# Six banks and spare products for the last pass of layer 3, run alone at the end of a four-layer kernel

## The chip, the cores and the metric

The kernel runs on one core of a Trainium2 chip. The core has five engines with a queue each: TensorE (PE; its weight loads are listed as PEld), VectorE (DVE), ScalarE (ACT), GpSimd (POOL) and SyncE (SP, here a queue of DMAs). Each queue is worked off strictly in the order in which the program was written; engines wait for one another by semaphores. The metric is the time of one execution in microseconds (us) on the device. TensorE's clock has two levels, 1.2 and 2.4 GHz; the profile shows the granted level as "PEclk", where 1.00 is 2.4 GHz and 0.50 is 1.2 GHz.

## The reference, cut to what matters

Four layers run one after the other on 64 sequences of 64 positions and 256 features. Layers 0 to 2 are attention layers (the last with a feed-forward part); layer 3 is a recurrent one:

```
xa  = ln(x); sx = shift(xa) - xa
xxx = tanh((xa + sx*maa_x) @ maa_w1)             # "maa"
xm_j = xa + sx*(maa_j + xxx_j @ maa_w2[j])       # "mix 0" to "mix 4": decay w, k, v, r, g
w   = exp(-exp(decay + tanh(xw@td_w1)@td_w2))    # "td", "decay"
k, v, r = xk@Wk.T, xv@Wv.T, xr@Wr.T;  g = silu(xg@Wg.T)
s_t = k_t v_t + w_t s_(t-1);  out_t = r_t (u k_t v_t + s_(t-1))   # "bonus", "scan"
x1  = x + groupnorm(out) * g @ Wo.T              # "center", "variance", "gate", "project"
xc  = ln(x1); xk2, xr2 = xc + sx2*ffn_k, xc + sx2*ffn_r
return x1 + sigmoid(xr2@Wfr.T) * (relu(xk2@Wfk.T)**2 @ Wfv.T)     # "ffn r", "ffn k", "ffn v"
```

All of it is in 32-bit floats.

## The kernel before, in words

The 64 sequences are worked in eight groups of eight (512 positions). Group g's layers 0 to 2 run in a block together with layer 3 of group g-1. The program of each engine is a list of steps of layers 0 to 2, and between them it calls `step()`, which emits the stages of layer 3 that are due there. Which stage is due at which step of which engine is a table written out by hand (`STAGES`, `PLACES`, `SCAN_PLACES`). The ninth block, number 8, has no group for layers 0 to 2 (`now` is None): each engine calls `rest()`, and layer 3 of the last group runs alone, stage after stage.

On TensorE the stages of layer 3 are, in order: turn, maa, mix 0, mix 1, td, k, mix 2, decay, v, mix 3, mix 4, r, g, bonus, 19 scan steps, center, variance, project, turn 2, ffn k, ffn r, ffn v. "maa" has four products of 128x512 (two of them in the first accumulation), a mix two products with a 32-row operand, td two, decay two with a 64-row operand, and k, v, r, g and ffn k four each. Project, ffn r and ffn v have eight products with 256 columns each. "turn" and "turn 2" are eight transposes of 128 columns. Every product in 32-bit floats is two MATMUL instructions in the profile (so four products are "x8"); a transpose is one.

TensorE's results go to eight PSUM banks, and the banks to rings (`RINGS`, line 71): "score" has banks 0 and 1, "turn" 2 to 5, "late" 6 and 7. `fill` takes the next bank of a ring for a tile, and waits until the tile that was there before has been read (`bank{b}_free`); the reader, ACT or DVE, waits for `bank{b}_full` in `take`. All of layer 3 goes through the ring "late", so a stage's third product waits until the first has been read. `product` (one or two accumulated products into one bank), `flip` (transposes) and `natural` (products with 256 columns, four to a bank) write a bank each.

Readers: ACT reads turn, maa, td, k, decay, v, r, g, center, variance, turn 2, ffn k and ffn r (mostly line 1047; L1090 for g, L1097 for center). DVE reads the mixes (L1307, then L1309 makes the mixed input xm), bonus, the scan's sums (L1334), project (L1387) and ffn v (L1408). The mixed inputs have two buffers. The stage g releases the DMAs of v (L666) that the scan needs; the scan itself is a chain between POOL (L1580), DVE (L1316, L1328) and a small product (L759).

Of the kernel before, what the change touches and what calls it, by code (L numbers as in the profile page):

```python
# [54 lines left out]
def build(nc, a, out):  # L55

    with ExitStack() as ctx:
# [5 lines left out]
        def sig(name):  # L63

            if name not in sems:
                sems[name] = ctx.enter_context(nc.semaphore(name))
            return sems[name]


        banks = [ctx.enter_context(nc.psum_tensor(f"bank{i}", [128, 512], F32)) for i in range(8)]  # L70
        RINGS = {"score": [0, 1], "turn": [2, 3, 4, 5], "late": [6, 7]}
        turns, fills, place, linked = {}, {}, {}, {}

        era = [None]
# [8 lines left out]
        def spot(tile):  # L83

            return place[era[0], tile]

        def fill(pe, ring, tile):

            b = RINGS[ring][turns.get(ring, 0) % len(RINGS[ring])]
            turns[ring] = turns.get(ring, 0) + 1  # L90
            n = fills.get(b, 0)
            if n:
                pe.wait_ge(sig(f"bank{b}_free"), n)
            fills[b] = n + 1
            place[era[0], tile] = (b, n + 1)
            return banks[b], sig(f"bank{b}_full")
# [430 lines left out]
        def clear_all():  # L527
# [60 lines left out]
        )  # L588
        due = {}
        for stage in STAGES:  # L590
            spots = SCAN_PLACES[stage[1]] if stage[0] == "scan" else PLACES[stage]
# [34 lines left out]
        def group_block(now, before, after):  # L626
# [45 lines left out]
            def tensor_program(pe):  # L672
# [3 lines left out]
                def product(tile, cols, terms, ring="turn"):  # L676

                    t, full = fill(pe, ring, tile)
                    for n, (lhsT, rhs) in enumerate(terms):
                        ins = mm(t[0:lhsT_cols(lhsT), 0:cols], lhsT, rhs, start=n == 0, stop=n == len(terms) - 1)  # L680
                    ins.then_inc(full, 1)

                def flip(tile, src, ring="turn"):

                    for k in range(KT):
                        t, full = fill(pe, ring, (tile, k))
                        for p in range(NP):
                            ins = tr(t[:, 128 * p:128 * p + 128], src[:, p, 128 * k:128 * k + 128], ident[:, :])
                        ins.then_inc(full, 1)

                def natural(tile, q, lhsT, rhs, ring="turn"):

                    t, full = fill(pe, ring, (tile, q))
                    for p in range(2):
                        for k, r in enumerate(rhs):
                            ins = mm(t[:, E * p:E * p + E], lhsT(2 * q + p, k), r, start=k == 0, stop=k == len(rhs) - 1)  # L696
                    ins.then_inc(full, 1)

                def layer3(stage):
                    def mix(f):  # L700
                        rows = slice(32 * (f % 4), 32 * (f % 4) + 32)
                        for m in range(KT):
                            product((stage, m), 512, [(maa2[rows, f // 4, 128 * m:128 * m + 128], xf[rows, f // 4, :])], "late")

                    def square(w, moving):
                        for m in range(KT):
                            product((stage, m), 512, [(wt[w][:, k, 128 * m:128 * m + 128], moving(k)) for k in range(KT)], "late")

                    def mixed(n, w):
                        pe.wait_ge(sig("xm_ready"), past("xm_ready") + KT * (n + 1))  # L710
                        square(w, lambda k: xm[:, (n + 1) % 2, k, :])

                    def project(w, moving):
                        for q in range(2):
                            natural(stage, q, lambda p, k: moving[:, k, 128 * p:128 * p + 128], [wt[w][:, k, :] for k in range(KT)], "late")

                    if stage == "turn":
                        pe.wait_ge(sig("xh3_ready"), past("xh3_ready") + NP)
                        flip(stage, xh3, "late")
                    elif stage == "maa":  # L720
                        pe.wait_ge(sig("x1m_ready"), past("x1m_ready") + KT)
                        product("maaA", 512, [(maa1[:, k, 0:128], xm[:, 0, k, :]) for k in range(KT)], "late")
                        product("maaB", 512, [(maa1[:, k, 128:160], xm[:, 0, k, :]) for k in range(KT)], "late")
                    elif stage[0:3] == "mix":
                        pe.wait_ge(sig("xf_ready"), past("xf_ready") + 2)
                        mix(MIXES[int(stage[4])])
                    elif stage == "td":
                        pe.wait_ge(sig("xm_ready"), past("xm_ready") + KT)
                        product("td", 512, [(td1[:, k, :], xm[:, 1, k, :]) for k in range(KT)], "late")
                    elif stage == "decay":  # L730
                        pe.wait_ge(sig("td_ready"), past("td_ready") + 1)
                        for m in range(KT):
                            product((stage, m), 512, [(td2[64:64 + DD, 128 * m:128 * m + 128], xf[64:64 + DD, 1, :])], "late")
                    elif stage == "k":
                        mixed(1, "Wk")
                    elif stage == "v":
                        mixed(2, "Wv")
                    elif stage == "r":
                        mixed(3, "Wr")
                    elif stage == "g":  # L740
                        mixed(4, "Wg")
                    elif stage == "bonus":
                        for k in range(KT):
                            pe.wait_ge(sig("ruk_ready"), past("ruk_ready") + k + 1)
                            product((stage, k), 512, [(heads8[:, :, :], ruk[:, k, :])], "late")
                    elif stage[0] == "scan":

                        n = stage[1] - 3
                        if 0 <= n < KT * HS and n % 2 == 1:
                            k, j = n // HS, n % HS  # L750
                            if j == 1:
                                t, full = fill(pe, "late", ("o3", k))
                            else:
                                b, c = spot(("o3", k))
                                t, full = banks[b], sig(f"bank{b}_full")
                            pe.wait_ge(sig("rs_ready"), past("rs_ready") + n + 1)
                            for i in (j - 1, j):
                                c, e = i % 4, i // 4
                                ins = mm(t[32 * c:32 * c + 32, :], pick[:, e, :, :], rs[:, i % RS, :], start=e == 0, stop=e == 1)  # L759
                            ins.then_inc(full if j == HS - 1 else sig("rs_used"), 1)  # L760
                    elif stage == "center":
                        for k in range(KT):
                            pe.wait_ge(sig("o3_ready"), past("o3_ready") + k + 1)
                            product((stage, k), 512, [(center8[:, :], ruk[:, k, :])], "late")
                    elif stage == "variance":
                        for k in range(KT):
                            pe.wait_ge(sig("sq_ready"), past("sq_ready") + k + 1)
                            product((stage, k), 512, [(same8[:, :, :], sq[:, k, :])], "late")
                    elif stage == "project":
                        pe.wait_ge(sig("ogT_ready"), past("ogT_ready") + KT)  # L770
                        project("Wo", ogT)
                    elif stage == "turn 2":
                        pe.wait_ge(sig("xh4_ready"), past("xh4_ready") + NP)
                        flip(stage, xh4, "late")
                    elif stage == "ffn k":
                        pe.wait_ge(sig("xk2_ready"), past("xk2_ready") + KT)
                        square("Wfk", lambda k: xk2[:, k, :])
                    elif stage == "ffn r":
                        pe.wait_ge(sig("xr2_ready"), past("xr2_ready") + KT)
                        project("Wfr", xr2)  # L780
                    elif stage == "ffn v":
                        pe.wait_ge(sig("kk_ready"), past("kk_ready") + KT)
                        project("Wfv", kkT)
# [928 lines left out]
```

## Time and profile before

| | us |
|---|---|
| median of 3 runs (lowest to highest) | 2005.09 (2001.06 to 2007.68) |
| the profiled execution | 2005.4 |
| its span | 2003.3 |
| PE busy (share of the span) | 1673.5 (84%) |
| DVE busy | 1275.2 (64%) |
| ACT busy | 931.7 (47%) |
| POOL busy | 801.7 (40%) |

The span is what the engines' records cover; 2.1 us lie around it. Times in the rows below are counted from the start of the span. An engine's busy share is a mean over parts of the program with different limits; the last 156 us, from 1847 on, are the block in which layer 3 runs alone.

### The profile page before, as it was taken

The page shows a single profiled execution, that of the slowest core. Times are in us where ns is not written, and L with a number is a line of the kernel's source. Part 1 is how long each engine was busy: PE and PEld are TensorE (multiplying, and loading weights), DVE is VectorE, ACT ScalarE, POOL GpSimd, SP SyncE. Part 2 cuts the span into 40 slices and gives each one's busy share as a digit, 9 for nine tenths or more (in the row PEclk, how much of TensorE's full clock was granted, in tenths as well). Part 3 has the DMA queues.
Part 4 walks back from the last instruction along what each step waited for, and adds up shares of the span by engine and source line. Part 5 has one row for each costly group of instructions (what it writes and reads, how often), then busy time and mean ns, then how long its engine had stood idle before and what let it go on. Part 6 is the DMA issues. An engine that isn't in the chain of part 4 may idle for free.

```text
span 2003.3 us, 36727 instructions
## 1 busy us (share of the span) xinstructions
PE 1673.5 (84%) x13614; PEld 1033.5 (52%) x13614; DVE 1275.2 (64%) x2181; ACT 931.7 (47%) x1831; POOL 801.7 (40%) x894
## 2 busy tenths in 40 slices
PE   3788898898988899798988989888987989888825
PEld 2465555564564645555555655546455555556203
DVE  3453468844796557854688457965589546883383
ACT  1555544545545444546445455454545454453202
POOL 3542137603474036611376024840367114760070
PEclk9899899999999999999989989999999999899757
DMA  6001005110241004210041102420042101410070
GB/s 175 1 2 35 1 7 59 24 41 4 29 49 38 18 1 54 34 27 18 10 56 23 38 7 25 52 39 18 1 55 34 27 18 14 52 24 12 0 85 11
DMA packets 73584, 60.92 MB, mean 30 GB/s; under 512 B 38961, under 2 KB 56513, under 8 KB 73409
## 3 DMA queue, kind: packets, MB, share of 16 engines
q1 hardware_dynamic: 49600, 41.70, 16.6%
q10 hardware_dynamic: 23264, 16.85, 3.0%
q8 instruction: 111, 1.82, 0.4%
q14 instruction: 65, 0.52, 0.1%
q0 software_dynamic: 544, 0.03, 0.0%
HBM read 20.28 MB, written 4.19 MB: 12 GB/s over the span
## 4 chain that ended last, share of the span: by engine, by line
PE 56%; ACT 15%; DVE 11%; issue 7%; POOL 6%; DMA 2%; ACTq 0%; DVEq 0%; POOLq 0%; SPq 0%
PE bank L680 24%; PE bank L819 6%; PE bank L1017 6%; PE bank L696 3%; PE bank L914 3%; PE bank L960 3%; ACT soft_ring L1156 3%; POOL soft_ring L1618 3%; DMA late<-late 2%; DVE late L1316 2%; PE bank L985 2%; PE bank L759 2%; ACT soft_ring L1175 2%; DVE soft_ring L1463 2%; ACT late L1047 2%
## 5 line engine op out<-in xcount | busy, mean ns | idle before, releaser
L1618 POOL TENSOR_TENSOR soft_ring<-soft_ring,seg_max 128x512 f32<-128x512 f32 x256 | 276.7, 1096 | 273.2 <-DVE seg_max L1469 272.5
L1175 ACT ACTIVATE soft_ring<-soft_ring 128x512 f32<-128x512 f32 x256 | 160.6, 627 | 228.5 <-POOL soft_ring L1618 216.0
L1580 POOL TENSOR_TENSOR late<-late 128x520 f32<-128x520 f32 x128 | 189.0, 1477 | 156.4 <-DMA late<-late 118.9
L1316 DVE TENSOR_TENSOR_SCAN late<-late 128x520 f32<-128x520 f32 x128 | 218.5, 1707 | 22.0 <-DVE xr L1494 6.7
L960 PE MATMUL bank<-ident,soft_ring 128*128 128x128 f32 x1024 | 170.0, 295 | 51.1 <-ACT soft_ring L1175 46.3
L1463 DVE SCALAR_TENSOR_TENSOR soft_ring<-bank,mask 128x512 f32<-128x512 f32 x256 | 164.2, 682 | 34.8 <-PE bank L819 25.7
L960 PEld LDWEIGHTS bank<-ident,soft_ring 128*128 128x128 f32 x1024 | 116.4, 147 | 135.0 <-ACT soft_ring L1175 83.7
L1469 DVE TENSOR_REDUCE seg_max<-soft_ring 128x8 f32<-128x512 f32 (+1 forms) x256 | 166.2, 675 | 6.2 <-DVE early L1527 2.0
L1626 POOL TENSOR_SCALAR soft_ring<-soft_ring,rden 128x256 f32<-128x256 f32 x64 | 61.6, 962 | 265.4 <-DVE rden L1436 265.4
L819 PE MATMUL bank<-early 64*128 64x512 f32 (+1 forms) x512 | 120.3, 556 | 56.4 <-ACTq L1159 53.6
L1047 ACT ACTIVATE late<-bank 128x512 f32<-128x512 f32 (+2 forms) x104 | 62.0, 596 | 204.4 <-PE bank L680 200.3
L680 PE MATMUL bank<-early,w 128*128 128x512 f32 x256 | 117.7, 610 | 17.9 <-ACT early L1234 17.9
L1589 POOL COPY late<-edge 128x8 f32<-128x8 f32 x16 | 3.2, 199 | 322.5 <-DVE late L1410 322.4
L680 PE MATMUL bank<-late,maa 32*128 32x512 f32 (+2 forms) x224 | 113.7, 631 | 9.0 <-ACTq L1049 5.1
L1017 PE MATMUL bank<-w,early 128*128 128x256 f32 x512 | 113.0, 379 | 0.0
L759 PE MATMUL bank<-late,pick 128*32 128x512 f32 x256 | 81.6, 721 | 36.7 <-DVE late L1328 36.7
L1307 DVE SCALAR_TENSOR_TENSOR late<-bank,vec,late 128x512 f32<-128x512 f32 x80 | 59.6, 745 | 75.0 <-PE bank L680 72.8
L1017 PEld LDWEIGHTS bank<-w,early 128*128 128x128 f32 x512 | 97.3, 190 | 16.6 <-issue 3.8
L819 PEld LDWEIGHTS bank<-early 64*128 64x128 f32 x512 | 49.3, 204 | 91.7 <-issue 84.7
L1328 DVE TENSOR_TENSOR late<-late 128x512 f32<-128x512 f32 x128 | 95.1, 748 | 0.0
L1582 POOL COPY late<-s 128x8 f32<-128x8 f32 x128 | 91.5, 715 | 8.1
L1047 ACT ACTIVATE early<-bank,vec 128x512 f32<-128x512 f32 x96 | 66.0, 688 | 61.0 <-PE bank L680 50.8
(246 smaller groups left out, 3357.6 us busy)
## 6 DMA issues: line engine op xcount, KB each, us to landing
late<-late SPq DMA_DIRECT2D x128, 260.0 KB, 4.4
c<-in_ctx ACTq DMA_DIRECT2D x8, 512.0 KB, 4.2
x<-in_x ACTq DMA_DIRECT2D x8, 512.0 KB, 5.2
out_x<-late SPq DMA_DIRECT2D x8, 512.0 KB, 2.9
mask<-in_mask_Bx1xSxS_ff ACTq DMA_DIRECT2D x16, 128.0 KB, 4.5
w<-in_L_xattn_mlp_w ACTq DMA_DIRECT2D x2, 1024.0 KB
mask<-in_mask_BxS_ik SPq DMA_DIRECT2D x8, 256.0 KB, 3.5
wkv<-in_L_xattn_kv_w ACTq DMA_DIRECT2D x1, 512.0 KB
```

What stands on the lines that cost most here:

```text
L680: ins = mm(t[0:lhsT_cols(lhsT), 0:cols], lhsT, rhs, start=n == 0, stop=n == len(terms) - 1)
L759: ins = mm(t[32 * c:32 * c + 32, :], pick[:, e, :, :], rs[:, i % RS, :], start=e == 0, stop=e == 1)
L819: ins = mm(t[:, width * n:width * n + width], lhsT, rhs, start=True, stop=True)
L960: ins = tr(t[:, 128 * n:128 * n + 128], soft[:, u % SOFT, 128 * n:128 * n + 128], ident[:, :])
L1017: ins = mm(t[:, E * (p % 2):E * (p % 2) + E], gT[:, k, 128 * p:128 * p + 128], w2[:, k, :], start=k == 0, stop=k == HID // 128 - 1)
L1047: link(af(dst, src(t), func, **kw))
L1175: af(soft[:, u % SOFT, :], soft[:, u % SOFT, :], ACT.Exp).then_inc(sig("exp"), 1)
L1316: nc.vector.tensor_tensor_scan(sj[:, n % 2, :], wP[:, k, :, :].rearrange("p b t -> p (b t)"), aj[:, n % 2, :], 0.0, ALU.mult, ALU.add).the ...
L1463: stt(out=cuts(u, soft[:, u % SOFT, :]), in0=cuts(u, t[:, :]), scalar=HD1 ** -0.5 if u < UNITS else 1.0 / HD2, in1=mask.unsqueeze(1).broad ...
L1469: nc.vector.tensor_reduce(seg_max[:, u % SOFT, 0:KVH if u < UNITS else 4], cuts(u, soft[:, u % SOFT, :]), X, ALU.max).then_inc(sig("max"), 1)
L1580: tt(aj[:, n % 2, :], kP[:, k, :, :].rearrange("p b t -> p (b t)"), vj[:, n % 3, :], ALU.mult).then_inc(sig("kv_done"), 1)
L1618: tt(s, s, seg_max[:, u % SOFT, 0:segs].unsqueeze(2).broadcast_to([128, segs, 512 // segs]), ALU.subtract).then_inc(sig("sub"), 1)
```

## The change

There is a new ring "all" of six banks: 6, 7 and the four of "turn". In the block where `now` is None, all of layer 3's products use it in place of "late" (`ring3`). In the other blocks nothing is changed.

In the same block, each stage of layer 3 on TensorE is preceded by `keep_busy(n)`: n products of the identity (128x128) with 256 columns of the weight matrix w1, all written over one another into one bank of the ring "score", which layer 3 doesn't use. Nobody reads them; TensorE itself counts the bank as free afterwards. They stand ahead of the stage's own wait, so they can run while its inputs are being made, but the stage's products come only after them. The table `BUSY` gives n by stage: 66 for turn to g and 61 for center to ffn v, 127 in all. "mix 1", "bonus" and the scan have none.

```diff
-        RINGS = {"score": [0, 1], "turn": [2, 3, 4, 5], "late": [6, 7]}
+        RINGS = {"score": [0, 1], "turn": [2, 3, 4, 5], "late": [6, 7], "all": [6, 7, 2, 3, 4, 5]}
...
+        BUSY = {"moments": 0, "turn": 10, "maa": 10, "mix 0": 8, "td": 6, "k": 4, "mix 2": 4, "decay": 4, "v": 4, "mix 3": 4,
+                "mix 4": 4, "r": 4, "g": 4, "center": 10, "variance": 8, "project": 10, "turn 2": 12, "ffn k": 10, "ffn r": 3,
+                "ffn v": 8}
...
+                ring3 = "late" if now is not None else "all"
+
+                def keep_busy(n):
+
+                    if n:
+                        t, full = fill(pe, "score", "spare")
+                        for _ in range(n):
+                            ins = mm(t[:, 0:E], ident[:, :], w1[:, 0, 0:E], start=True, stop=True)
+                        ins.then_inc(full, 1)
+                        pe.sem_inc(sig(f"bank{spot('spare')[0]}_free"), 1)
+
                 def layer3(stage):
                     def mix(f):
                         rows = slice(32 * (f % 4), 32 * (f % 4) + 32)
                         for m in range(KT):
-                            product((stage, m), 512, [(maa2[rows, f // 4, 128 * m:128 * m + 128], xf[rows, f // 4, :])], "late")
+                            product((stage, m), 512, [(maa2[rows, f // 4, 128 * m:128 * m + 128], xf[rows, f // 4, :])], ring3)
...
+                    if now is None:
+                        keep_busy(BUSY.get(stage, 0))
                     if stage == "turn":
                         pe.wait_ge(sig("xh3_ready"), past("xh3_ready") + NP)
-                        flip(stage, xh3, "late")
+                        flip(stage, xh3, ring3)
```

The other changed lines put `ring3` in the place of "late" in the same way.

## Rows read from the trace of the kernel before

**Rows 1.** The page: PEclk in 40 slices; a group (count | busy, mean ns | idle).
```profile
PEclk9899899999999999999989989999999999899757
...
L1307 DVE SCALAR_TENSOR_TENSOR late<-bank,vec,late 128x512 f32<-128x512 f32 x80 | 59.6, 745 | 75.0 <-PE bank L680 72.8
```

**Rows 2.** Timeline of PE, 1800 to 1852: start, us, line, tiles, count.
```profile
1821.70 7.07 PE L1017 MATMUL bank<-w,early 128*128 128x256 f32 x32
1828.61 3.60 PE L680 MATMUL bank<-late,t_Wfk 128*128 128x512 f32 x8
1832.04 3.62 PE L696 MATMUL bank<-t_Wfr,late 128*128 128x256 f32 x16
...
1851.69 1.97 PE L688 MATMUL bank<-ident,late 128*128 128x128 f32 x8 [4.79 <-DVE late L1297]
```

**Rows 3.** Timeline of PE, last block up to g; brackets: idle before, and its releaser.
```profile
1856.78 5.25 PE L680 MATMUL bank<-late,maa 128*128 128x512 f32 x8 [3.12 <-DVE late L1349]
1862.83 3.21 PE L680 MATMUL bank<-late,maa 32*128 32x512 f32 x6 [0.80 <-ACTq L1049]
...
1868.23 3.68 PE L680 MATMUL bank<-late,td 128*64 128x512 f32 x4
1871.83 4.43 PE L680 MATMUL bank<-late,t_Wk 128*128 128x512 f32 x8
```

**Rows 4.** Chain that ended last: start, us, what; the pieces that end stages.
```profile
1832.24 0.61 ACT late L1047
...
1862.06 0.60 ACT late L1047
...
1902.47 0.61 ACT late L1090
...
1959.03 0.60 ACT late L1097
...
1962.89 0.70 ACT late L1047
...
1974.12 0.70 DVE late L1387
...
1990.59 0.61 ACT late L1047
...
1994.65 3.71 PE bank L696 x16
```

**Rows 5.** Windows of 1 to 6 us: busy us by engine, then PEclk, DMA.
```profile
1859.00:1860.00 1.00, 1.00 (x2) 0.00 (x0) 0.00 (x0) 0.00 (x0) 0.00 (x0) 0.66 0.00 0
...
1867.00:1873.00 6.00, 6.00 (x8) 1.41 (x7) 2.78 (x5) 0.59 (x1) 0.00 (x0) 0.50 0.01 3
...
...
1891.00:1897.00 6.00, 6.00 (x8) 2.02 (x8) 3.71 (x6) 0.00 (x0) 0.00 (x0) 0.50 0.00 0
...
1989.00:1990.00 1.00, 1.00 (x4) 0.37 (x3) 0.00 (x0) 0.00 (x0) 0.00 (x0) 0.80 0.00 0
```

**Rows 6.** Timeline of PE after the scan.
```profile
1955.25 1.92 PE L759 MATMUL bank<-late,pick 128*32 128x512 f32 x4 [0.61 <-DVE late L1328]
1957.10 2.75 PE L680 MATMUL bank<-late,center 128*128 128x512 f32 x4
...
1968.46 5.62 PE L696 MATMUL bank<-t_Wo,late 128*128 128x256 f32 x16 [5.75 <-DVE late L1382]
1978.87 1.73 PE L688 MATMUL bank<-ident,late 128*128 128x128 f32 x8 [4.79 <-DVE late L1297]
1984.38 6.18 PE L680 MATMUL bank<-late,t_Wfk 128*128 128x512 f32 x8 [3.78 <-DVE late L1401]
```

**Rows 7.** Waits of PE from 1846.8: total us, times, longest.
```profile
PE bank L680 <- DVEq L1308: 1.0, 4, 0.3
PE bank L680 <- ACTq L1049: 0.8, 1, 0.8
PE bank L696 <- ACTq L1048: 0.6, 1, 0.6
```

More of the change, by code:

```diff
@@ L702, in mix @@
                         for m in range(KT):
-                            product((stage, m), 512, [(maa2[rows, f // 4, 128 * m:128 * m + 128], xf[rows, f // 4, :])], "late")
+                            product((stage, m), 512, [(maa2[rows, f // 4, 128 * m:128 * m + 128], xf[rows, f // 4, :])], ring3)
                     def square(w, moving):
                         for m in range(KT):
-                            product((stage, m), 512, [(wt[w][:, k, 128 * m:128 * m + 128], moving(k)) for k in range(KT)], "late")
+                            product((stage, m), 512, [(wt[w][:, k, 128 * m:128 * m + 128], moving(k)) for k in range(KT)], ring3)
                     def mixed(n, w):
@@ L714, in project @@
                         for q in range(2):
-                            natural(stage, q, lambda p, k: moving[:, k, 128 * p:128 * p + 128], [wt[w][:, k, :] for k in range(KT)], "late")
+                            natural(stage, q, lambda p, k: moving[:, k, 128 * p:128 * p + 128], [wt[w][:, k, :] for k in range(KT)], ring3)
+                    if now is None:
+                        keep_busy(BUSY.get(stage, 0))
                     if stage == "turn":
                         pe.wait_ge(sig("xh3_ready"), past("xh3_ready") + NP)
-                        flip(stage, xh3, "late")
+                        flip(stage, xh3, ring3)
                     elif stage == "maa":
                         pe.wait_ge(sig("x1m_ready"), past("x1m_ready") + KT)
-                        product("maaA", 512, [(maa1[:, k, 0:128], xm[:, 0, k, :]) for k in range(KT)], "late")
-                        product("maaB", 512, [(maa1[:, k, 128:160], xm[:, 0, k, :]) for k in range(KT)], "late")
+                        product("maaA", 512, [(maa1[:, k, 0:128], xm[:, 0, k, :]) for k in range(KT)], ring3)
+                        product("maaB", 512, [(maa1[:, k, 128:160], xm[:, 0, k, :]) for k in range(KT)], ring3)
                     elif stage[0:3] == "mix":
@@ L728, in layer3 @@
                         pe.wait_ge(sig("xm_ready"), past("xm_ready") + KT)
-                        product("td", 512, [(td1[:, k, :], xm[:, 1, k, :]) for k in range(KT)], "late")
+                        product("td", 512, [(td1[:, k, :], xm[:, 1, k, :]) for k in range(KT)], ring3)
                     elif stage == "decay":
@@ L732, in layer3 @@
                         for m in range(KT):
-                            product((stage, m), 512, [(td2[64:64 + DD, 128 * m:128 * m + 128], xf[64:64 + DD, 1, :])], "late")
+                            product((stage, m), 512, [(td2[64:64 + DD, 128 * m:128 * m + 128], xf[64:64 + DD, 1, :])], ring3)
                     elif stage == "k":
@@ L744, in layer3 @@
                             pe.wait_ge(sig("ruk_ready"), past("ruk_ready") + k + 1)
-                            product((stage, k), 512, [(heads8[:, :, :], ruk[:, k, :])], "late")
+                            product((stage, k), 512, [(heads8[:, :, :], ruk[:, k, :])], ring3)
                     elif stage[0] == "scan":
@@ L751, in layer3 @@
                             if j == 1:
-                                t, full = fill(pe, "late", ("o3", k))
+                                t, full = fill(pe, ring3, ("o3", k))
                             else:
@@ L763, in layer3 @@
                             pe.wait_ge(sig("o3_ready"), past("o3_ready") + k + 1)
-                            product((stage, k), 512, [(center8[:, :], ruk[:, k, :])], "late")
+                            product((stage, k), 512, [(center8[:, :], ruk[:, k, :])], ring3)
                     elif stage == "variance":
@@ L767, in layer3 @@
                             pe.wait_ge(sig("sq_ready"), past("sq_ready") + k + 1)
-                            product((stage, k), 512, [(same8[:, :, :], sq[:, k, :])], "late")
+                            product((stage, k), 512, [(same8[:, :, :], sq[:, k, :])], ring3)
                     elif stage == "project":
@@ L773, in layer3 @@
                         pe.wait_ge(sig("xh4_ready"), past("xh4_ready") + NP)
-                        flip(stage, xh4, "late")
+                        flip(stage, xh4, ring3)
                     elif stage == "ffn k":
```

## The prediction

> **What bounds the kernel now.** The page comes first: its slices of the clock stand at 0.8 to 0.9 and more for most of the span and fall to 0.7, 0.5 and 0.7 in the last three slices [rows 1], some 150 us. There layer 3 of the last group runs alone, and only there does the change act, so everything before 1846.9 stays. Next comes the chain that ended last, with TensorE's timeline beside it. The reader is to see three parts. Up to g (1902.47) the chain is nearly all TensorE: it idles 4.79 us before turn, 3.12 before maa and 0.80 before mix 0 [rows 2, 3], and from mix 0 on hardly at all; the waits for a bank that DVE or ACT still reads come to 1.0 us in four pieces, with 0.6 us at ffn v [rows 7]. From g to the end of the scan (1902.47 to 1955.25) a DMA, POOL and DVE set the time, which the change doesn't touch. After the scan TensorE idles 5.75 us before project, 4.79 before turn 2 and 3.78 before ffn k, and works at the low clock for much of the rest [rows 6].
>
> So two things can be gained: the low clock while TensorE works, and 1.6 us of waits for banks. Price of a product: at the full clock four with 512 columns take 1832.04 - 1828.61 = 3.43 us, 0.858 each, and sixteen with 256 columns 1828.61 - 1821.70 = 6.91, 0.432 each [rows 2]. At the low clock two with 512 columns take 1871.83 - 1868.23 = 3.60 [rows 3], about 1.7 to 1.8 each, twice as much.
>
> **The change part by part.** A spare product is a full 32-bit product with 256 columns: 0.432 us at the full clock, 0.86 at the low one. 127 of them are 55 us. What covers them is only idle time ahead of the same stage, since TensorE's queue is in order: a spare product that isn't done when the stage's inputs are ready delays it. I go through the stages, first with the full clock wherever TensorE has been kept busy.
>
> Turn: 10 are 4.32 us, inside the 4.79 of idle; start unchanged at 1851.69. Eight transposes with 128 columns at the full clock are half of the low clock's 1.7 to 2.0, 0.86.
>
> Maa: 1851.69 + 0.86 + 10 x 0.432 = 1856.87, against 1856.78; its inputs would be ready some 0.4 earlier, but the spare products are not done. Shift +0.1.
>
> Mix 0: maa's four products, 3.43 at the full clock, end at 1860.30; the second read comes 3.63 after the start (as 1832.24 - 1828.61, [rows 2, 4]) at 1860.50, and mix 0 may follow 1862.83 - 1862.06 = 0.77 later [rows 3, 4], at 1861.27. But 8 spare products run to 1863.76. Shift +0.93; the full clock's gain in maa (1.65) is more than spent.
>
> Mix 0 to g: 30 real products with 512 columns (mixes 10, td 2, k 4, decay 2, v 4, r 4, g 4) are 25.74 us. Six banks let them follow without a wait. 38 spare ones (6 at td, 4 at each of eight stages) are 16.42. No input ends later than TensorE gets there: for td, mix 0's two results take DVE about 3 us (0.745 each [rows 1] and an addition of like size), while TensorE has mix 0, mix 1 and six spare products, 6.0 us, in between. Sum 42.16, and 0.20 to the read of g's second half: 1863.76 + 42.36 = 1906.12, against 1902.47 [rows 4]. Shift +3.65. Before, this stretch took 39.64, with the low clock in three windows of 6 us, of which the first and the last stand in [rows 5]; the spare products cost more than those three did.
>
> The clock there: each time, it had fallen after the mixes and decay, whose operands have 32 or 64 rows, though TensorE was busy all the time (6.00 of 6.00, at 0.50) [rows 5]. Now mix 0 and mix 1 still stand together, 3.43 us of such products, between full ones; elsewhere spare products stand between. Bounds: no fall, 0; or a fall with 6 us at half speed, 3.0 us, up to three, 9.0. I take half of one, +1.5, since only one of the three places keeps its form.
>
> The Trainium skill ("TensorE: Matmul & The Clock Gate", § Why this matters for your kernels) says to have no idle gaps longer than about 3 us between bursts of products so that the clock stays up. By that rule alone no fall would come in this stretch, and the sum below would be 1.5 us less; the low clock at full busy shares speaks against taking it alone.
>
> Scan: it starts with the DMA that g releases, and takes as long as before.
>
> Center: its 10 spare products begin at 1957.10 at the low clock. The clock rose 2.9 us (1859.7) and 4.8 us (1989.2) after products began at 1856.78 and 1984.38 [rows 3, 5, 6]; counted from the last scan product, 1955.25, that is 1958.2 to 1960.1. With 1959.1, 2.0 us are cold and do 2.34 products, the other 7.66 take 3.31: 5.3 us. Center starts at C = 1962.4, was 1957.10. None of it is covered: center's inputs were ready.
>
> Variance: center's two products 1.72, 8 spare ones 3.46, first product and read 1.06: C + 6.24 = 1968.64, against 1962.89 [rows 4]. Shift +5.75. (The table load, which set this read before, is over at C + 1.06 + 3.86 = C + 4.92.)
>
> Project: its inputs come 1968.46 - 1962.89 = 5.57 later, at 1974.21; the spare products are done at C + 6.90 + 4.32 = 1973.62, covered. Warm, its second half is read after 3.63 instead of 1974.12 - 1968.46 = 5.66: at 1977.84. Shift +3.7.
>
> Turn 2: inputs 4.75 later (1978.87 - 1974.12), 1982.59; 12 spare products end at 1974.21 + 3.46 + 5.18 = 1982.85. Ffn k: 0.86 + 4.32 = 5.18 on, 1988.03, against 1984.38: +3.65. Its four products are warm, so the second read comes after 3.63 and not 6.21: 1991.66 against 1990.59 [rows 4], +1.07.
>
> Ffn r and ffn v: TensorE is free at 1991.46; 3 spare products 1.30, ffn r 3.46, 8 spare ones 3.46: ffn v starts at 1999.68, against 1994.65 [rows 4]. Shift +5.03, which holds to the end. Its cover was only the 0.6 us of wait for a bank.
>
> The trace shows no semaphore step of TensorE for itself (19 of them) and no product whose bank nobody reads. Lower bound of such a step 0; upper the longest of those four waits, 0.3 each, 5.7 in all; I take 0, since the pieces between instructions on the chain are hundredths.
>
> Sum: 3.65 + 1.5 + 5.03 = +10.2 on the profiled execution's 2005.4 (span 2003.3 and 2.1 around it): 2015.6. That execution is 0.3 above the median of the three runs, so the forecast is 2015.3.
>
> **Rivals.** (a) A spare product costs half, 0.216, because its neighbours load the same identity and nothing accumulates. Then turn, maa, project, turn 2 and ffn k are covered with room; mix 0 starts at 1861.54 and g is read 34.15 later, at 1895.7 (-6.8); after the scan variance's read comes 2.3 later, and project (-2.0), ffn k (-3.0) and ffn v (+1.6) make it -1.1. Sum -8: 1997. The point from which it decides: between +8.7 (without the fall) and -8 the sum is nought at 0.32 us per spare product. For it: no row shows such a product. Against: the 32 instructions of L1017 with 256 columns need 0.216 each, and a product is two [rows 2]. Chance 0.05.
>
> The skill's page ("TensorE: Matmul & The Clock Gate", § Back-to-back issue gap) gives columns / 2.4 GHz + 2.5 ns, 109 ns for 256 columns and 0.22 us for two instructions, an estimate by it that would make rival (a) true; the rows have twice that for each instruction in 32-bit floats, and they decide.
>
> (b) The clock falls again and again in the stretch up to g, as before: mixes with 32 rows pull it down in spite of 4 full products between them. Three falls of 3.0 us instead of half a one: +7.5, 2022.8. For it: three of three mix pairs did so. Against: each pair now has full products between its halves, but for the first. Chance 0.15.
>
> (c) No measurable change: no fall, center's clock rising at once (-0.4), and a profiled execution of the kernel before that had one fall more, 3.0, than they have in the mean (three runs lie 6.6 us apart): 2005.1 + 8.7 - 0.4 - 3.0 = 2010.4. The place is the same, the sum only just reaches the bound. Chance 0.12.
>
> **How the numbers follow.** The forecast as worked out 0.68, (a) 0.05, (b) 0.15, (c) 0.12. 0.3% of 2005.1 is 6.0 us, about what a measurement of this kernel can tell from no change. Faster is (a), 0.04 beyond that bound; within it half of (c) and a little of the rest, 0.12; slower 0.84. The range goes from (c), with 2.4 us for where the clock's changes fall, to (b): 2008 to 2023.
>
> **What would show each step.** TensorE's timeline of the last block: spare groups of x20 at 4.3 us, not 2.2, decide between the forecast and (a). Mix 0 starts about 1 us later than 1862.83 and its four products follow without idle; g's second read lies near 1906 to 1908, in an interval without idle on TensorE. Windows there show 1.00, but for a piece near td. Center starts 5 us later after its last scan product than before; project and ffn k take 3.5 us instead of 5.6 and 6.2; ffn v starts 8.0 us after ffn k's second read, not 4.1. The prediction is wrong if g comes earlier than 1902, or if stages overtake their spare products.

## The result and the profile after

The changed kernel takes 2016.37 us (median of 6 runs, 2012.86 to 2018.69), the kernel before beside it 2005.65 (6 runs, 2001.06 to 2007.68): a ratio of 1.0054, 95% interval 1.0042 to 1.0066. It is slower by 10.7 us. The forecast was 2015.3 in a range of 2008 to 2023.

The page of the changed kernel, lines that answer to [rows 1]:

```profile
span 2014.1 us, 37254 instructions
...
PE 1710.7 (85%) x13868; PEld 1074.9 (53%) x13868; DVE 1276.0 (63%) x2181; ACT 930.8 (46%) x1831; POOL 804.0 (40%) x894
...
PEclk9899899999998899999998999989989999999959
```

The last three slices of the clock stood at 7, 5 and 7, and now at 9, 5 and 9, and the span is 10.8 us longer: TensorE runs nearly all of the last block at the full clock, except in the scan and for the first 4 us behind it, and the kernel is slower. TensorE has 254 instructions more (13868 against 13614), which are the 127 spare products.

The timeline of PE in the changed kernel, last block up to g; it answers to [rows 3]. L709 is a spare product, L683 a real one:

```profile
1846.57 4.48 PE L709 MATMUL bank<-w,ident 128*128 128x256 f32 x20
1851.52 1.09 PE L691 MATMUL bank<-ident,late 128*128 128x128 f32 x8 [0.47 <-DVE late L1313]
1852.45 4.48 PE L709 MATMUL bank<-w,ident 128*128 128x256 f32 x20
1856.77 3.71 PE L683 MATMUL bank<-late,maa 128*128 128x512 f32 x8
1860.41 3.72 PE L709 MATMUL bank<-w,ident 128*128 128x256 f32 x16
1864.06 1.99 PE L683 MATMUL bank<-late,maa 32*128 32x512 f32 x8
1865.98 2.86 PE L709 MATMUL bank<-w,ident 128*128 128x256 f32 x12
1868.77 1.93 PE L683 MATMUL bank<-late,td 128*64 128x512 f32 x4
1870.63 1.99 PE L709 MATMUL bank<-w,ident 128*128 128x256 f32 x8
1872.46 3.60 PE L683 MATMUL bank<-late,t_Wk 128*128 128x512 f32 x8
1875.90 1.89 PE L709 MATMUL bank<-w,ident 128*128 128x256 f32 x8
1877.72 1.98 PE L683 MATMUL bank<-late,maa 32*128 32x512 f32 x4
1879.63 1.99 PE L709 MATMUL bank<-w,ident 128*128 128x256 f32 x8
```

And after the scan, answering to [rows 6]:

```profile
1959.67 1.92 PE L775 MATMUL bank<-late,pick 128*32 128x512 f32 x4 [0.60 <-DVE late L1344]
1961.52 6.67 PE L709 MATMUL bank<-w,ident 128*128 128x256 f32 x20
1968.03 1.88 PE L683 MATMUL bank<-late,center 128*128 128x512 f32 x4
1969.74 3.62 PE L709 MATMUL bank<-w,ident 128*128 128x256 f32 x16
1973.20 1.88 PE L683 MATMUL bank<-late,same 128*128 128x512 f32 x4
1974.91 4.48 PE L709 MATMUL bank<-w,ident 128*128 128x256 f32 x20
1979.83 3.72 PE L699 MATMUL bank<-t_Wo,late 128*128 128x256 f32 x16 [0.43 <-DVE late L1398]
1983.38 5.34 PE L709 MATMUL bank<-w,ident 128*128 128x256 f32 x24
1988.56 1.04 PE L691 MATMUL bank<-ident,late 128*128 128x128 f32 x8
1989.44 4.48 PE L709 MATMUL bank<-w,ident 128*128 128x256 f32 x20
1993.80 3.70 PE L683 MATMUL bank<-late,t_Wfk 128*128 128x512 f32 x8
...
2002.09 3.62 PE L709 MATMUL bank<-w,ident 128*128 128x256 f32 x16
2005.54 3.62 PE L699 MATMUL bank<-t_Wfv,late 128*128 128x256 f32 x16
```

The numbers in brackets are what to look for: they are the time that TensorE sat idle before a group. In the two stretches together there are three short ones. Before, turn, maa, project, turn 2 and ffn k each waited 3 to 6 us for DVE, and now the spare products stand there and end 0.4 us early or just too late. Ahead of center, variance and ffn v, where nothing had waited for long, spare products stand as well, and push everything behind them.

The two reads by ACT that end stages in the changed kernel, answering to 1902.47 and 1962.89 of [rows 4] (g's second half, variance's first):

```profile
1906.91 0.60 ACT L1106 ACTIVATE late<-bank 128x512 f32<-128x512 f32 x1 [0.49 <-PE bank L683]
...
1974.26 0.69 ACT L1063 ACTIVATE late<-bank,eps 128x512 f32<-128x512 f32 x1 [1.32 <-PE bank L683]
```

Windows of the changed kernel (PEclk is the third number from the end), answering to [rows 5]:

```profile
1868.00:1873.00 5.00, 5.00 (x18) 2.77 (x18) 3.02 (x5) 0.59 (x1) 0.00 (x0) 1.00 0.00 0
1890.00:1896.00 6.00, 6.00 (x19) 2.95 (x17) 3.19 (x5) 0.00 (x0) 0.00 (x0) 1.00 0.00 0
...
1962.00:1965.00 3.00, 3.00 (x8) 2.38 (x8) 0.33 (x1) 0.00 (x0) 0.32 (x2) 0.50 0.00 0
1966.00:1968.00 2.00, 2.00 (x11) 1.77 (x10) 0.00 (x0) 0.00 (x0) 0.00 (x0) 1.00 0.00 0
```

Two distances carry the rest of this text, because the block's start differs by some us from execution to execution. **A** is the time from mix 0's first product to ACT's read of g's second half; before 1902.47 - 1862.83 = 39.64, after 1906.91 - 1864.06 = 42.85. **B** is the time from the last scan product to ffn v's first product; before 1994.65 - 1955.25 = 39.40, after 2005.54 - 1959.67 = 45.87. They hold +3.2 and +6.5; the way to mix 0 (from DVE's read at 1846.93 and 1846.77) went from 15.90 to 17.29, +1.4. Sum +11.1.

### The profile page after: what moved, and what is told of

Same layout as the page of the kernel before. It is cut to its first block, busy times and chain, and to the rows that moved or that the text cites. A ratio compares the mean times of both kernels' runs of the same rounds, so it can differ in the third digit from the quotient of the medians.

```text
span 2014.1 us, 37254 instructions
## 1 busy us (share of the span) xinstructions
PE 1710.7 (85%) x13868; PEld 1074.9 (53%) x13868; DVE 1276.0 (63%) x2181; ACT 930.8 (46%) x1831; POOL 804.0 (40%) x894
## 3 DMA queue, kind: packets, MB, share of 16 engines
q1 hardware_dynamic: 49600, 41.70, 16.4%
## 4 chain that ended last, share of the span: by engine, by line
PE 57%; ACT 14%; DVE 11%; issue 7%; POOL 6%; DMA 2%; ACTq 0%; DVEq 0%; POOLq 0%; SPq 0%
PE bank L683 23%; PE bank L835 6%; PE bank L1033 5%; PE bank L699 3%; PE bank L930 3%; PE bank L976 3%; ACT soft_ring L1172 3%; POOL soft_ring L1634 2%; PE bank L709 2%; DVE late L1332 2%; DMA late<-late 2%; PE bank L1001 2%; PE bank L775 2%; ACT soft_ring L1191 2%; DVE soft_ring L1479 2%
## 5 line engine op out<-in xcount | busy, mean ns | idle before, releaser
L683 PE MATMUL bank<-early,w 128*128 128x512 f32 x256 | 124.4, 639 | 17.9 <-ACT early L1250 17.9
L683 PE MATMUL bank<-late,maa 32*128 32x512 f32 (+2 forms) x224 | 107.6, 611 | 3.2 <-ACTq L1065 3.1
L1448 DVE TENSOR_REDUCE nmax<-bank 128x2 f32<-128x512 f32 x64 | 42.9, 684 | 83.0 <-PE bank L835 81.0
```

## The experiments

Each kernel was timed in 5 rounds beside the kernel before on the same chip, but for e8, which was run once. The three groups of kernels ran on three chips, and the median of the kernel before was 2005.9, 2005.7 and 2003.9 there, so the ratios are what is compared; A and B are from the one profiled execution of each. The edits are against the changed kernel, cut to the lines that count.

| kernel | median us | ratio to before (95%) | A | B |
|---|---|---|---|---|
| before | 2005.65 | 1 | 39.64 | 39.40 |
| the change | 2016.37 | 1.0054 (1.0042 to 1.0066) | 42.85 | 45.87 |
| e1, banks only | 1997.10 | 0.9953 (0.9934 to 0.9972) | 32.52 | 38.95 |
| e2, spare products only | 2019.85 | 1.0068 (1.0047 to 1.0089) | 45.51 | 44.39 |
| e3, half the columns | 2003.95 | 0.9989 (0.9978 to 1.0001) | 36.02 | 39.34 |
| e5, none from td to g | 2005.16 | 1.0001 (0.9988 to 1.0013) | 32.51 | 44.79 |
| e10, none at center, variance, ffn r, ffn v | 2004.91 | 1.0003 (0.9989 to 1.0017) | 42.85 | 34.34 |
| e6, 32 rows | 2023.45 | 1.0091 (1.0070 to 1.0112) | 56.84 | 44.95 |
| e8, banks only, same rows | 1995.06 (one run) | | 32.52 | 38.95 |
| e4, only under idle time | 1992.76 | 0.9932 (0.9915 to 0.9949) | 34.77 | 34.05 |
| e7, e4 with td 4 and r 5 | 1987.44 | 0.9913 (0.9894 to 0.9932) | 30.49 | 32.96 |
| e9, e7 with the scan | 1990.57 | 0.9922 (0.9904 to 0.9940) | 30.49 | 34.61 |

**e1_banks_only**: which half of the change costs?

```diff
-        BUSY = {"moments": 0, "turn": 10, "maa": 10, "mix 0": 8, "td": 6, "k": 4, "mix 2": 4, "decay": 4, "v": 4, "mix 3": 4,
-                "mix 4": 4, "r": 4, "g": 4, "center": 10, "variance": 8, "project": 10, "turn 2": 12, "ffn k": 10, "ffn r": 3,
-                "ffn v": 8}
+        BUSY = {}
```

> Six banks, no spare product. Theory: the spare products cost all of the 10.7 us and the ring is a small gain, the 1.6 us of waits for banks and perhaps a clock that falls less often: 2002 to 2004, g's second read 1 to 3 us earlier than in the kernel before. Rival: the ring of six itself costs something (banks given back in another order, readers late): 2008 or more.

The loss is the spare products', as both the sign and the ratio show. But the size is a miss: the forecast was 2002 to 2004, 1 to 3 us under the kernel before, and 0.9953 is some 9 us. A fell by 7.1 us and B by 0.45. The timeline of PE of this kernel at the mixes:

```profile
1865.81 2.06 PE L681 MATMUL bank<-late,maa 32*128 32x512 f32 x8 [0.80 <-ACTq L1063]
1870.11 3.40 PE L681 MATMUL bank<-late,td 128*64 128x512 f32 x4 [2.24 <-DVE late L1323]
...
1885.08 1.99 PE L681 MATMUL bank<-late,maa 32*128 32x512 f32 x8
1889.46 5.40 PE L681 MATMUL bank<-late,t_Wr 128*128 128x512 f32 x8 [2.39 <-DVE late L1323]
```

Eight instructions, the four products of two mixes, take 2.0 us, where four products with 512 columns take 3.43. With a bank each they run side by side (e8 tests this); before, six of them took 3.21 and the last two waited for DVE [rows 3]. TensorE is then so early that it waits for DVE instead. Before, windows of 1 us show the low clock within A three times for 6.8 us, some 20 in all (the prediction counted 6 for each); here they show it from 1869.7 to 1873.1 and from 1890.2 to 1893.6, 6.8 us in all.

**e2_spares_only**: the other half alone.

```diff
-                ring3 = "late" if now is not None else "all"
+                ring3 = "late"
```

> The 127 spare products, layer 3 still on two banks. Theory: the loss is theirs, and the ring only hid waits: mix 1 waits for DVE again (0.5 us) and most other waits lie under spare products: 2016 to 2018. Rival (the ring costs): 2005 to 2010.

2019.85, above the theory's 2016 to 2018; the interval of its ratio, 1.0047 to 1.0089, holds the change's, so the two aren't told apart by time. A says more: 45.51 against 42.85, 2.7 us, which is the one place where two mixes stand together in both (1868.01 - 1863.43 = 4.58 us, in place of 1865.98 - 1864.06 = 1.92):

```profile
1863.43 3.21 PE L681 MATMUL bank<-late,maa 32*128 32x512 f32 x6
1866.96 1.12 PE L681 MATMUL bank<-late,maa 32*128 32x512 f32 x2 [0.32 <-DVEq L1322]
```

So the ring is worth 9 us without the spare products and some 3 with them (by A): they keep mix 3 and mix 4 apart, and the clock is 1.00 in all of e2's A without the ring, so little is left for it to bring.

**e3_half_columns**: what does a spare product's price depend on?

```diff
-                            ins = mm(t[:, 0:E], ident[:, :], w1[:, 0, 0:E], start=True, stop=True)
+                            ins = mm(t[:, 0:128], ident[:, :], w1[:, 0, 0:128], start=True, stop=True)
```

> The change with spare products of 128 columns in place of 256, so 0.216 us each. Theory (a spare product costs its columns, and what has no cover is lost one for one): the sum that was made for this price in the prediction's rival, -8 us, a little less where the clock now falls: 1997 to 2001. Rival (each spare product, or each group of them, has a fixed price that its columns do not set): 2010 or more.

2003.95, 0.9989: between the two. The price does follow the columns: turn's group of twenty instructions lasts 2.39 us in place of 4.48. The forecast of -8 missed two things. A is 36.02, not 34.15: the group of eight before a stage takes 0.9 to 1.15 us, not 0.86. And 10 or 12 short products no longer fill the waits of 4.8 to 5.8 us: TensorE idled 2.55 us before turn, 2.88 before project and 2.11 before turn 2, and the clock fell at each. Windows of this kernel, the low clock in each:

```profile
1857.00:1860.00 3.00, 3.00 (x16) 3.00 (x16) 2.67 (x4) 2.08 (x3) 0.00 (x0) 0.50 0.00 0
1970.00:1972.00 2.00, 2.00 (x6) 1.55 (x6) 0.00 (x0) 0.00 (x0) 0.00 (x0) 0.50 0.00 0
1980.00:1983.00 3.00, 3.00 (x17) 3.00 (x15) 1.91 (x3) 1.55 (x2) 0.00 (x0) 0.50 0.00 0
```

**e5_no_mid** and **e10_no_late**: where in the block is the loss? Each takes a part of the change back.

```diff
+        BUSY = {'turn': 10, 'maa': 10, 'mix 0': 8, 'center': 10, 'variance': 8, 'project': 10, 'turn 2': 12, 'ffn k': 10, 'ffn r': 3, 'ffn v': 8}   # e5
+        BUSY = {'turn': 10, 'maa': 10, 'mix 0': 8, 'td': 6, 'k': 4, 'mix 2': 4, 'decay': 4, 'v': 4, 'mix 3': 4, 'mix 4': 4, 'r': 4, 'g': 4, 'project': 10, 'turn 2': 12, 'ffn k': 10}   # e10
```

> The change without the 38 spare products ahead of td to g; the 8 of mix 0 and all after the scan stay. Theory (in this stretch they cost their 16.4 us, and give back the clock's falls and DVE's waits that come without them): mix 0 to g's second read goes from 42.85 us to the 32.5 to 34.8 of the kernels without them, -8 to -10 from the change, 2006 to 2008.5. Rival (no clock was gained by them here at all): -16, 2000.

> The change without the spare products ahead of center, variance, ffn r and ffn v; the others stay. Theory (nothing covers these 29; project keeps the full clock by its own 10): variance's read 7 us earlier, ffn v 4.7 us earlier, so -11 to -12 from the change, 2004 to 2006. Rival (without them the clock falls before project or center stays cold for longer, and half of it is lost again): 2009 to 2011.

Both near their theory's figures and far from their rivals'. Without the 38 ahead of td to g the ratio goes from 1.0054 to 1.0001, some 10.6 us where 8 to 10 were forecast, and A from 42.85 to 32.51; without the 29 ahead of center, variance, ffn r and ffn v it goes to 1.0003, some 10.2 us where 11 to 12 were forecast, and B from 45.87 to 34.34. Each takes back about 10 us; 38 products are 16.4 us by their price, and 10.3 of A were lost net, so the full clock and the absence of waits repaid 6.

**e6_32_rows**: does idle time alone lower the clock?

```diff
-                            ins = mm(t[:, 0:E], ident[:, :], w1[:, 0, 0:E], start=True, stop=True)
+                            ins = mm(t[:, 0:E], ident[0:32, :], w1[0:32, 0, 0:E], start=True, stop=True) if stage in ("mix 0", "td", "k", "mix 2", "decay", "v", "mix 3", "mix 4", "r", "g") else mm(t[:, 0:E], ident[:, :], w1[:, 0, 0:E], start=True, stop=True)
```

> The change, with the spare products ahead of mix 0, td to g made on 32 rows of the identity and of w1 in place of 128; same number, same columns. Theory (the clock falls under products that use few rows, busy or not): the clock falls at least twice between mix 0 and g, although TensorE is never idle there, and g's second read comes 3 to 10 us later: 2019 to 2026. Rival (only idle time lowers the clock; the spare products held it by filling the idle time): 1.00 all through, 2014 to 2017.

2023.45, as the theory had it, and the clock fell three times between mix 0 and g, with TensorE busy throughout. Windows of this kernel:

```profile
1867.00:1887.00 20.00, 20.00 (x35) 9.86 (x33) 5.12 (x8) 1.19 (x2) 0.00 (x0) 0.50 0.00 0
1889.00:1893.00 4.00, 4.00 (x21) 2.88 (x20) 2.36 (x4) 0.05 (x1) 0.00 (x0) 1.00 0.00 0
1895.00:1900.00 5.00, 5.00 (x10) 2.52 (x9) 0.00 (x0) 0.89 (x2) 0.00 (x0) 0.50 0.00 0
1909.00:1914.00 5.00, 5.00 (x10) 2.74 (x9) 1.74 (x3) 0.00 (x0) 0.00 (x0) 0.50 0.00 0
```

Busy for 20.00 of 20.00 us at half speed: the rival, idle time alone, is out. A little over half of these 20 us (11.3) is products with 32 rows; the rest is td and most of k, with 128. Some of these spare products also ran side by side with a mix on other rows, so this kernel lost by the clock although some of its products cost less than their price. Its profiled execution (2030.6) is the slowest of six, and A = 56.84 is for that one.

**e8_same_rows**: is it the rows that let the mixes run side by side? Mix 1 and mix 4 are replaced by second copies of mix 0's and mix 3's products.

```diff
+        BUSY = {}
...
+                        if now is None:
+                            f = {0: 1, 4: 3}.get(f, f)
```

> Six banks, no spare product, and mix 1 and mix 4 take the operands of mix 0 and mix 3, so that neighbouring mixes stand on the same 32 rows (this leaves the real products of mix 1 and mix 4 out). Theory (products on different groups of 32 rows run side by side, once each has a bank): the group of eight instructions takes 3.5 to 3.9 us in place of 2.0. Rival (the six banks alone make them short, whatever rows they use): 2.0 again. The time changes little, since DVE reads the four results for 6 us in either case: within 4 us of the kernel with banks only.

```profile
1860.34 3.69 PE L681 MATMUL bank<-late,maa 32*128 32x512 f32 x8 [0.80 <-ACTq L1065]
1864.64 3.41 PE L681 MATMUL bank<-late,td 128*64 128x512 f32 x4 [0.61 <-DVE late L1325]
```

3.69 in place of 2.06, and the wait behind it shrinks from 2.24 to 0.61: td starts at 4.30 us after mix 0 in both. A and B are those of e1, 32.52 and 38.95; the one execution took 1995.1 us. So the rows make the mixes short, but in these two kernels DVE's four reads hide it; what e1 gains in A comes from the banks' waits and from the clock.

**e4_covered_only**: can the idle time alone pay for the clock?

```diff
+        BUSY = {'turn': 10, 'maa': 8, 'mix 0': 1, 'project': 11, 'turn 2': 10, 'ffn k': 9}
```

> Six banks, and spare products only as many as fit in the idle time ahead of a stage: turn 10, maa 8, mix 0 1, project 11, turn 2 10, ffn k 9; none elsewhere. Theory: maa, project and ffn k run at the full clock at no price: -2 at maa, -1 for the banks up to g, -2.0 at project, -3.0 at turn 2 and ffn k, -0.6 at ffn v; 1996 to 1998. Rival (the clock is only held by spare products that stand in the way of the real ones; those under idle time do not raise it): 2003 to 2005.

1992.76, 0.9932, lower than the forecast 1996 to 1998: A fell by 4.9 us against the kernel before, where 1 was put down to the banks. B is 34.05, 4.9 less than with banks only (38.95). In A the clock fell after the two mixes and the wait behind them, and k ran at the low clock, so A is worse than e1's:

```profile
1867.74 2.35 PE L681 MATMUL bank<-late,td 128*64 128x512 f32 x4 [2.24 <-DVE late L1323]
1870.74 6.27 PE L681 MATMUL bank<-late,t_Wk 128*128 128x512 f32 x8 [0.65 <-DVE late L1323]
```

**e7_covered_mid**: spare products in the two waits that e1 showed.

```diff
+        BUSY = {'turn': 10, 'maa': 8, 'mix 0': 1, 'td': 4, 'r': 5, 'project': 11, 'turn 2': 10, 'ffn k': 9}
```

> The kernel with spare products under idle time only, plus 4 ahead of td and 5 ahead of r, where TensorE waits 2.24 and 2.39 us for DVE. Theory (two side-by-side mixes and the wait behind them made the clock fall; 1.7 and 2.2 us of full products inside the wait hold it): k takes 3.7 us in place of 6.3 and r 3.6 in place of 5.4, 1987 to 1990. Rival (4 are too few, the clock falls anyway, and the spare products are then slow ones in the way): 1992 to 1996.

```profile
1856.62 2.06 PE L681 MATMUL bank<-late,maa 32*128 32x512 f32 x8 [0.17 <-ACTq L1063]
1858.61 1.99 PE L707 MATMUL bank<-w,ident 128*128 128x256 f32 x8
1860.92 1.93 PE L681 MATMUL bank<-late,td 128*64 128x512 f32 x4 [0.32 <-DVE late L1323]
1863.92 3.70 PE L681 MATMUL bank<-late,t_Wk 128*128 128x512 f32 x8 [1.07 <-DVE late L1323]
```

And its window of the whole stretch:

```profile
1857.00:1888.00 31.00, 28.17 (x78) 12.12 (x74) 13.80 (x20) 8.75 (x15) 0.00 (x0) 1.00 0.00 0
```

1987.44, the lowest median of all and within the forecast, 0.9913 (0.9894 to 0.9932), 17 us under the kernel before by its ratio. td starts 4.30 us after mix 0 as in e1, so the four products cost nothing, and the clock is full in all of A, though TensorE is busy for 28.17 of 31 us only. It has 58 spare products where the change had 127. B is 1.1 less than e4's, with the same spare products after g: in e7 the clock rose at 1941.1, 0.4 us before center began, and in e4 1.7 us after it, which is not the edit's doing. The intervals of e7's and e4's ratios overlap, so the times don't tell the two apart, and the profiled executions are the fastest of e7's six and the slowest of e4's. What speaks for the edit is A: 30.49 against 34.77, and 30.49 again in e9, another kernel with the same spare products up to g.

**e9_scan_cover**: the clock ahead of center.

```diff
+        BUSY = {'turn': 10, 'maa': 8, 'mix 0': 1, 'td': 4, 'r': 5, 'project': 11, 'turn 2': 10, 'ffn k': 9, ('scan', 14): 4, ('scan', 16): 5}
```

> As the kernel with td 4 and r 5, plus 4 and 5 spare products ahead of the sixth and seventh pair of scan products, where TensorE waits 3.7 us for DVE each time. Theory: the last scan products and center run at the full clock, -1.0 and -0.9 us, if the spare products (3.5 to 4.3 us at the low clock) fit: 1.5 to 2 us less than that kernel. Rival (they do not fit at the low clock and hold up the scan's products, whose buffers DVE needs): equal or later by up to 2 us.

No gain that shows: 1990.57, 0.9922, an interval that holds e7's ratio, and B 34.61 against 32.96. The spare products fitted: the scan's products came at the same distances as in e7 (5.6, 5.6 and 2.5 us), and two groups of them took 1.12 and 1.05 us in place of 1.92. But then TensorE waited twice, 2.17 and 1.48 us:

```profile
1945.90 1.05 PE L773 MATMUL bank<-late,pick 128*32 128x512 f32 x4 [2.17 <-DVE late L1342]
1948.43 1.92 PE L773 MATMUL bank<-late,pick 128*32 128x512 f32 x4 [1.48 <-DVE late L1342]
```

The clock had risen at 1940.4 and fell at 1947.3, in the second of these waits, and was down again for the last scan products and center. That is a third outcome, which neither theory named: the clock was raised too early to last until center.

## Why the prediction was right

The mechanism was right. A spare product costs 0.43 us in an in-order queue unless TensorE would have waited there anyway, and the full clock gives back less than that. Rival (a), the half price, is ruled out: groups of twenty instructions take 4.3 us at the full clock from their start to the next (1856.77 - 1852.45). Rival (b), repeated falls, did not come: 1.00 in all windows of 1 us between mix 0 and g, in the changed kernel and again in e10, which is the same up to there. For (c) the result is too large, with the lower end of the interval 8.4 us above.

By steps, shifts against the prediction's own (less the 0.16 us by which the block began earlier):

- Turn at 1851.52 and maa at 1856.77: forecast 1851.69 and 1856.87. Right to 0.1.
- Mix 0 at 1864.06, which is 1864.22 with the 0.16, forecast 1863.76: 0.46 late. Maa's group (3.64 us to the next start) and that of the 16 spare instructions behind it (3.65) are each 0.2 longer than 3.43 and 3.46.
- A: forecast 42.36 at the full clock and 1.5 for a fall, 43.86; measured 42.85. Three terms were off and cancelled in part. The fall didn't come (-1.5). Mix 0 and mix 1 took 1.92 us and not 3.43 (-1.5), since they run side by side; the prediction took each product as a step of its own. And every change of form costs: eight spare instructions take 1.83 ahead of k and not 1.73, a mix between spare products 1.91 and not 1.72, +2.0 over the stretch from the end of the two mixes to the end of g's products (1903.28 + 3.43 - 1865.98 = 40.73, against 26 x 0.858 + 38 x 0.432 = 38.72).
- Center: after the last scan product it started 8.36 us later, forecast 7.15. The clock rose at 1965.8, 6.1 us after that product, and not 3.8; the ten spare products took 6.51 us in place of 5.3. The prediction had bounds of 2.9 and 4.8 from two other stages (finer windows put that rise at 1989.4, so 5.0), and passed over the rise at this very place in the kernel before: at 1958.7, 3.4 after the last scan product. In the other kernels without spare products in the scan it comes 1.1 (e3) to 4.2 us (e6) after it. So the middle was well placed, but the bounds were too narrow. The three other kernels with the same 61 spare products after the scan have B 44.39, 44.79 and 44.95 (e2, e5, e6; rises after 3.1, 3.9 and 4.2 us), against the forecast's 39.40 + 5.03 = 44.43: what is above that in the changed kernel goes with the late rise in its one execution.
- Variance's read, +6.95 after the last scan product in place of +5.75; all of the 1.2 is center's.
- Project 5.57 after that read, turn 2 8.73 after project (8.64), ffn k 5.24 after turn 2 (5.18), ffn v 11.74 after ffn k (11.65). Right to 0.1 each. The step of TensorE's semaphore for itself was put at nothing, and no idle time stands behind any group of spare products.

Sum of the misses: +0.46 - 1.5 - 1.5 + 2.0 + 1.2 and some tenths, +0.9, and so 10.2 became 11.1 within the block. The total was closer than its terms, and that is luck: three of them are 1.5 to 2 us off and cancel.

What the prediction missed in kind is the ring: it had 1.6 us of waits for it. Alone it is worth 9 us (e1): A loses the waits for banks and two thirds of its time at the low clock (6.8 us of it against some 20; half of the difference, 6.8 us, is an estimate of what that is worth). The spare products leave little of that gain. That the clock falls less often and for a shorter time with the ring is seen in the windows; why was not tried, and stays open.

The Trainium skill ("TensorE: Matmul & The Clock Gate", § Part 3: Packing small matmuls — row/col tiling) says that products on different groups of 32 rows run together. The traces agree: eight instructions take 1.92 to 2.06 us, against 3.69 on the same rows (e8).

The Trainium skill ("TensorE: Matmul & The Clock Gate", § Why this matters for your kernels) asks that there be no long idle gaps between bursts of products, with the length that the prediction quotes. By that rule alone no fall was due here, and none came. But it is not enough: the clock fell in e6 with no gap at all, and in e1 with waits of 2.24 and 2.39 us, shorter than that length. e7's gaps, up to 1.1 us, are within it too, and there the clock stayed up.

## What to carry to other kernels

Work that only keeps TensorE's clock up is free where the engine would wait anyway. Anywhere else it costs its full price, and only a part of that came back here (some 6 of 16 us between td and g, in clock and waits): count it against the idle time of each stage in the trace, not against the engine's mean. Where the stages are bound by TensorE itself, take its waits for banks away first, and read again: here the two longest waits that appeared then were places where four and five spare products held the clock for nothing. Where a change has two parts, undo each by itself; this one's good half (0.9953) was buried under its bad one (1.0068).

## What was not expected of the hardware

- Four products of 32 rows and 512 columns, on two groups of rows and with a bank each, take 1.92 us; on one group 3.69.
- The clock fell to 1.2 GHz and stayed there for 20 us of unbroken work, a little over half of it products with 32 rows of operand (e6); the same number of products with 128 rows held it at 2.4 GHz.
- In the changed kernel it rose 6.1 us after the start of the last scan product, in the kernel before 3.4, and in e7 and e4, whose spare products after r are the same, 1.2 and 3.6. In the eleven traces with nothing changed in the scan it comes after 1.1 to 6.1 us: where it rises moves by some us from execution to execution. Six runs of one kernel lie 6 to 12 us apart; how much of that is the clock was not measured.
- Between products of different form some 0.1 us is lost at each change: a mix (32 rows) or decay (64) between spare products takes 1.91 us and td (64 columns) 1.86, against 1.72 for two products with 512 columns; between groups of one form, as from r's spare products on to g, nothing is lost.
